# The four projections of a batch as three fp32r products, with the contexts split by GpSimd

## What is computed

```python
x = x + tanh(g_xattn[0]) * xattn(layernorm(x), ctx, ctx)      # 16 heads of 16 dimensions
x = x + tanh(g_ffn[0]) * moe(layernorm(x))                    # 8 experts, the best 2 of each token

def xattn(q, k, v):
    qh, kh, vh = q @ w_q.T + b_q, k @ w_k.T + b_k, v @ w_v.T + b_v    # the projections Q, K, V
    attn = softmax(qh @ kh.T / sqrt(16))                              # for each head
    return (attn @ vh) @ w_o.T + b_o                                  # the projection of the output
```

## Time and profile before

| what | value |
|---|---|
| median of 3 runs | 1241.16 us (1239.86 to 1241.84) |
| the profiled execution | 1240.26 us, span of its records 1238.4 us |
| granted TensorE clock, mean over the span | 0.959 of full |
| busy: PE, DVE, ACT, POOL | 1118.4, 643.7, 555.2, 312.8 us |
| instructions | 24933 |

### The profile page before, as it was taken

One profiled execution on the slowest core, in us unless ns is written; L12 is line 12 of the kernel. 1 busy time (PEld: TensorE's weight loads), 2 busy tenths in 40 slices (PEclk: granted clock), 3 DMA queues, 4 the chain that ended last, 5 costly groups with the idle time before them and its releaser, 6 DMA issues. The chain is left out here.

```text
span 1238.4 us, 24933 instructions
## 1 busy us (share of the span) xinstructions
PE 1118.4 (90%) x8725; PEld 949.4 (77%) x8725; DVE 643.7 (52%) x1524; ACT 555.2 (45%) x890; POOL 312.8 (25%) x366
## 2 busy tenths in 40 slices
PE   5789999999999998449999999999979999999994
PEld 4566666666666665326789999999948999999994
DVE  2546777776667766427643444444455444434442
ACT  3456666666666665236533333333354333333331
POOL 2122444444443332312212211121121221122111
PEclk8889999999999998669999999999989999999997
DMA  9100111011111101176342211221141221122111
GB/s 305 49 11 19 46 36 35 35 40 44 41 44 35 35 28 36 46 305 239 101 161 35 35 31 22 35 35 31 30 126 28 35 34 31 22 35 35 31 22 26
DMA packets 47642, 73.39 MB, mean 59 GB/s; under 512 B 6256, under 2 KB 42352, under 8 KB 44400
## 3 DMA queue, kind: packets, MB, share of 16 engines
q0 software_dynamic: 16896, 43.53, 13.7%
q1 hardware_dynamic: 29616, 28.21, 7.6%
q10 hardware_dynamic: 1088, 1.11, 0.3%
HBM read 47.66 MB, written 24.90 MB: 59 GB/s over the span
## 5 line engine op out<-in xcount | busy, mean ns | idle before, releaser
L1468 POOL DMA_INDIRECT out<-y,token x64 | 101.4, 1585 | 475.0 <-DVE y L1404 379.1
L1332 ACT ACTIVATE silu<-gate 128x512 f32<-128x512 f32 x128 | 76.5, 598 | 281.0 <-PE up L1241 281.0
L1398 DVE TENSOR_TENSOR h<-silu,up 128x512 f32<-128x512 f32 x128 | 88.0, 687 | 195.9 <-ACT silu L1332 195.9
L854 DVE TENSOR_REDUCE max_neg<-maxps 128x4 f32<-128x1024 f32 x128 | 156.4, 1222 | 58.3 <-PE maxps L468 56.7
L656 ACT ACTIVATE probs<-scores 128x1024 f32<-128x1024 f32 x128 | 131.8, 1030 | 68.1 <-PE scores L487 68.1
L1253 PE MATMUL down<-w_hi,h_hi 128*128 128x256 f32 x512 | 146.9, 287 | 0.0
L1253 PE MATMUL down<-w_hi,h_lo 128*128 128x256 f32 x512 | 144.1, 281 | 0.0
L1253 PE MATMUL down<-w_lo,h_hi 128*128 128x256 f32 x512 | 143.8, 281 | 0.0
L1400 DVE TENSOR_TENSOR h_lo<-h,h_hi 128x512 fp32r<-128x512 f32 x128 | 88.6, 692 | 89.4 <-ACT h_hi L1335 89.4
L1335 ACT ACTIVATE h_hi<-h 128x512 fp32r<-128x512 f32 x128 | 80.9, 632 | 96.5 <-DVE h L1398 96.5
L1241 PE MATMUL gate<-x_hi,w_hi 128*128 128x256 f32 x512 | 103.1, 283 | 0.0
(11 more groups left out here) (165 smaller groups left out, 2258.7 us busy)
## 6 DMA issues: line engine op xcount, KB each, us to landing
xg<-dispatched SPq DMA_DIRECT2D x41, 272.0 KB, 2.7
stage<-gate_T POOLq DMA_DIRECT2D x8, 1024.0 KB, 7.7
stage<-up_T POOLq DMA_DIRECT2D x8, 1024.0 KB, 9.6
stage<-down_T POOLq DMA_DIRECT2D x8, 1024.0 KB, 12.0
x_all<-x SPq DMA_DIRECT2D x16, 256.0 KB, 6.9
ctxT<-ctxT SPq DMA_DIRECT2D x16, 256.0 KB, 2.7
out<-x_all SPq DMA_DIRECT2D x16, 256.0 KB, 2.1
out<-y,token POOLq DMA_INDIRECT x72, 3.8
```

The source lines that it names most:

```text
L854: V.tensor_reduce(to, maxps[:], AX.X, ALU.max, negate=True).then_inc(s["max_taken"], 1)
L1332: nc.scalar.activation(silu[pair % 2][:], gate[pair % 2][:], ACT.Silu).then_inc(s_silu, 1)
L1398: V.tensor_tensor(h[pair % 2][:], silu[pair % 2][:], up[pair % 2][:], ALU.mult).then_inc(s_made, 1)
L1468: pool.indirect_dma_start(out, bass.IndirectOffsetOnAxis(token[:, t:t + 1], axis=0), y[:, t, :], None, compute_op=ALU.add).then_inc(s_adde ...
```

## The change

The weights of the four projections are split in the prologue, by VectorE, between the row maxima of the first batch; TensorE waits for all four before its first body. In the bodies V (except the first), K, Q and the output projection are twelve fp32r products each instead of four plain ones. The context is split by GpSimd at the head of its body. The high parts of the turned x and of the turned output are written by ScalarE where it copied them before, and the rests by VectorE, which reads the PSUM bank again and sets it free. In the loop SyncE waits for the split of an earlier context instead of for TensorE. `oT` goes; sixteen tensors are new in SBUF. Scores, softmax, routing and experts stay. The diff, cut to its core:

```diff
@@ SyncE, body @@
                 if ahead:
-                    sp.wait_ge(s["misc_written"], use.before)
+                    if isinstance(b, int):
+                        sp.wait_ge(s["misc_written"], use.before)
+                    else:
+                        sp.wait_ge(s["ctx_split"], b - 1)
                     load_ctx(b + 2, par)
@@ TensorE @@
+            def three_terms(high, rest, high2, rest2):
+                return [(l, r, c) for l, r in ((high, high2), (high, rest2), (rest, high2)) for c in range(HC)]
+
+            def project_in_parts(w, high2, rest2, what, use):
+                use.free(pe, what)
+                terms = three_terms(w_high[w], w_rest[w], high2, rest2)
+                for o in range(HC):
+                    for n, (l, r, c) in enumerate(terms):
+                        last = mm(use.bank(what)[:, o, :], l[:, c, o * P:(o + 1) * P], r[:, c, :], start=n == 0, stop=n == len(terms) - 1)
+                last.then_inc(s["misc_written"], 1)
...
+            def project_q_in_parts(use):
+                use.read(pe, "TX")
+                project_in_parts("q", x_high, x_rest, "Q", use)
+
+            def project_k_in_parts(b, par, use):
+                pe.wait_ge(s["ctx_split"], b - 1)
+                project_in_parts("k", c_high[par], c_rest[par], "K", use)
+
+            def project_v_in_parts(par, use):
+                rows_in_parts(c_high[par], c_rest[par], "v", "V", use)
@@ attn_out @@
                 use.read(pe, "TN")
-                use.free(pe, "WO")
...
+                rows_in_parts(o_high, o_rest, "o", "WO", use)
@@ before the bodies @@
+            pe.wait_ge(s["w_split"], 4)
             over_batches(pe, body)
@@ ScalarE @@
+            def high_of(to, what, made, use):
+                use.written(act, what)
+                nc.scalar.activation(to[:], use.bank(what)[:], ACT.Copy).then_inc(s[made], 1)
...
-                    read_whole(xT[:], "TX", use)
+                    high_of(x_high, "TX", "x_high_made", use)
                 exps(b, 2)
                 if back:
-                    read_whole(oT[:], "TN", use)
+                    high_of(o_high, "TN", "o_high_made", use)
@@ VectorE @@
+            def rest_of(b, to, high_, what, made, use):
+                dve.wait_ge(s[made], b)
+                V.tensor_tensor(to[:], use.bank(what)[:], high_[:].bitcast(fp32), ALU.subtract).then_inc(use.freed(what), 1)
+
+            def split_weights(n, what, raw):
+                V.tensor_copy(w_high[what][:], raw[:]).then_inc(s["w_high_made"], 1)
+                dve.wait_ge(s["w_high_made"], n + 1)
+                V.tensor_tensor(w_rest[what][:], raw[:], w_high[what][:].bitcast(fp32), ALU.subtract).then_inc(s["w_split"], 1)
@@ prologue, after the maxima of each pair @@
+                if pair >= 4:
+                    split_weights(pair - 4, "kvqo"[pair - 4], (wk_s, wv_s, wq_s, wo_s)[pair - 4])
@@ body @@
                 max_of_next(2)
+                if ahead:
+                    rest_of(b + 1, x_rest, x_high, "TX", "x_high_made", use)
+                if back:
+                    rest_of(b, o_rest, o_high, "TN", "o_high_made", use)
                 if late:
                     first_choice(b - 2)
                 max_of_next(3)
@@ GpSimd @@
+            def split_ctx(b, par):
+                if isinstance(b, int):
+                    pool.wait_ge(s["ctx_loaded"], b * 16 + 16)
+                else:
+                    alone.wait_ge(s["ctx_loaded"], b * 16 + 16)
+                G.tensor_copy(c_high[par][:], cT[par][:]).then_inc(s["ctx_high_made"], 1)
+                alone.wait_ge(s["ctx_high_made"], b - 1)
+                G.tensor_tensor(c_rest[par][:], cT[par][:], c_high[par][:].bitcast(fp32), ALU.subtract).then_inc(s["ctx_split"], 1)
@@ body @@
                 if ahead:
+                    if not is_first(b):
+                        alone.wait_ge(s["misc_written"], use.before - 3)
+                    split_ctx(b + 2, par)
                     scale_x(b + 2)
                     split(b + 2, "K", use, units_before(b) + (UNITS.index("K1") + 1 - len(UNITS)))
```

More of the change, by code:

```diff
@@ L123, in attention_stage @@
         wo_s = sb("wo_s", [P, HC, D])
+        w_high = {what: sb(f"w{what}_high", [P, HC, D], f32r) for what in "qkvo"}
+        w_rest = {what: sb(f"w{what}_rest", [P, HC, D], f32r) for what in "qkvo"}
+        c_high = [sb(f"ctx_high{i}", [P, HC, SEQ], f32r) for i in range(2)]
+        c_rest = [sb(f"ctx_rest{i}", [P, HC, SEQ], f32r) for i in range(2)]
+        x_high = sb("x_high", [P, HC, SEQ], f32r)
+        x_rest = sb("x_rest", [P, HC, SEQ], f32r)
+        o_high = sb("o_high", [P, HC, SEQ], f32r)
+        o_rest = sb("o_rest", [P, HC, SEQ], f32r)
         bq_s = sb("bq_s", [P, HC])
@@ L164, in attention_stage @@
         on = sb("on", [P, QT, D])
-        oT = sb("oT", [P, HC, SEQ])
         row = [sb(f"row{i}", [P, QT, ROW]) for i in range(2)]
@@ L201, in attention_stage @@
             rows_chain rows_ready scattered count_chain counted values_made
-            scale_chain scale2_chain""".split()
+            scale_chain scale2_chain ctx_high_made ctx_split w_high_made w_split
+            x_high_made o_high_made""".split()
         s = {n: sem(n) for n in names}
@@ L440, in project_v, with rows_in_parts @@
                 last.then_inc(s["misc_written"], 1)
+            def three_terms(high, rest, high2, rest2):
[7 more added lines that the diff above has]
+                last.then_inc(s["misc_written"], 1)
+            def rows_in_parts(high, rest, w, what, use):
+                use.free(pe, what)
+                terms = three_terms(high, rest, w_high[w], w_rest[w])
+                for t in range(QT):
+                    for n, (l, r, c) in enumerate(terms):
+                        last = mm(use.bank(what)[:, t, :], l[:, c, t * P:(t + 1) * P], r[:, c, :], start=n == 0, stop=n == len(terms) - 1)
+                last.then_inc(s["misc_written"], 1)
+            def project_q_in_parts(use):
[6 more added lines that the diff above has]
+                rows_in_parts(c_high[par], c_rest[par], "v", "V", use)
             def write_unit(n):
@@ L579, in stack_ahead @@
                         stack(b + 2, what[0], int(what[1]), unit(b, what))
-                if nxt:
+                if is_first(b):
                     project_v(1 - par, use)
+                elif nxt:
+                    project_v_in_parts(1 - par, use)
                 max_of_next(0)
@@ L590, in body @@
                 if ahead:
-                    project_k(b + 2, par, use)
+                    project_k_in_parts(b + 2, par, use)
                 score(b, par, 1)
@@ L611, in body @@
                 if ahead:
-                    project_q(use)
+                    project_q_in_parts(use)
                 max_of_next(5)
@@ L779, in _ @@
             over_batches(act, body)
-            read_whole(oT[:], "TN", EPILOGUE)
+            high_of(o_high, "TN", "o_high_made", EPILOGUE)
             second_weight(BATCHES - 2)
@@ L997, in _ @@
             norm_heads(b, 1, EPILOGUE)
+            rest_of(BATCHES, o_rest, o_high, "TN", "o_high_made", EPILOGUE)
             first_choice(b - 1)
```

## The result

| | before | after |
|---|---|---|
| median | 1241.50 us (1239.86 to 1242.87, 4 runs) | 1312.93 us (1311.18 to 1317.77, 4 runs) |
| the profiled execution | 1240.26 us, span 1238.4 | 1311.18 us, span 1309.3 |
| granted TensorE clock | 0.959 | 0.930 |

The ratio is 1.0585 (95% interval 1.0558 to 1.0613). The forecast was 1310 in a range of 1272 to 1328. A time "in the turn" counts from the first record of the turn's product V. Lines L... are those of the kernel in question.

The account below looks back on a forecast made before the run. TensorE was taken to bound the attention stage. To 1240.3 us came 14 x 3.0 = 42 for longer turns, 13 x 2.0 = 26 for the clock and 2.2 for edges: 70 more, 1310, range 1272 to 1328.

Parts of the forecast that it names:

- TensorE's gain: Projections as twelve fp32r products: 0.5 us less for K, Q and WO, 0.4 for V, 1.9 a turn.
- GpSimd: Context split ahead of scale_x delays xn and exponentials: 2.5 us stall before the second scores, which come 1.65 later.
- VectorE: Rests between maxima of pairs 2 and 3 delay WO, first_choice and masks: ranks 3.5 us late, turn 3.0 longer.
- the rule that I weighed: VectorE instructions with two SBUF inputs and GpSimd SBUF reads exclude each other; rests with a PSUM operand stay unaffected.
- The clock: TensorE's waits lower its clock in every turn: 2.0 us each in 13 turns, 26 us.
- the sign of being right: Attention stage: a turn of 32 to 35 us would show the forecast right.
- The edges: Prologue's last weight split 1.1 us, as much again for the first turn, last turns and epilogue 0: 2.2 us.
- No fall of the clock: Rival: attention turns lengthen but the clock stays up; 1285 us (1274 to 1303), chance 0.28.
- Only one chain is real: Rival: context split earlier or rests delay nobody; about 0.5 us a turn, 1247 to 1250, chance 0.11.
- The faster rival: TensorE's saving stands if first exponentials end by 258.9 and maxima 3 come early; 1212 us, chance 0.06.

Follow-up runs that it names:

- e2: Changed kernel with scale_x put before the split of the context on GpSimd, nothing else: 1281.83 us.
- e4: Changed kernel with only K and V in three fp32r products, Q and output projection plain, no rests on VectorE: 1271.19 us.
- e10: Changed kernel with contexts loaded one turn earlier, ahead of the transfers of the maxima, rests left in place: 1279.63 us.
- e8: Changed kernel with the two rests behind first_choice on VectorE, nothing else: 1288.63 us.
- e9: Changed kernel with contexts loaded a turn ahead and the rests behind first_choice, output projection in its old place: 1263.23 us.
- e1: Changed kernel with products nobody reads filling TensorE's waits before the second scores, maxima of pair 4 and ranks: 1290.80 us.
- e5: As e4, but each context loaded a turn ahead and only the weights of K and V split: 1237.85 us.
- e6: As e5, plus Q in parts with both parts of x made by GpSimd behind the split of K: 1238.22 us.
- e3: Changed kernel with only Q and output projection in parts; K and V plain, no context split, SyncE's old wait: 1290.38 us.
- e7: Changed kernel with contexts loaded a turn ahead, rests behind first_choice, output projection behind the scores of pair 4: 1261.35 us.
- e12: As e7, with products nobody reads in TensorE's two waits, before weighted values 0 and scores of pair 4: 1246.67 us.

## Why the prediction was right

Set beside turn 7, us into the turn:

| step | as predicted | measured |
|---|---|---|
| split of the context ends | 3.7 | 3.68 |
| `scale_x` begins | 3.9 | 3.76 |
| xn begins | 5.8 | 5.72 |
| second scores, after a wait of | 7.9, 2.5 | 7.77, 2.08 |
| output projection | 12.9 | 12.73 |
| maxima of pair 3 | 14.5 | 14.42 |
| waits before maxima of pair 4 and ranks | 1.1 and 1.1 | 0.83 and 0.90 |
| ranks | 17.2 | 17.10 |
| the turn, against before | +3.0 | +3.08 |

- **TensorE's gain.** This term was too large. Pairs of the new products start 0.24 us apart, 0.12 each, as taken from the earlier trace rows, but the first pair (except in V) and the step to the next group take 0.33 us each. From the start of the group to that of the next the output projection takes 1.63 us (300.50 to 302.13) and V 1.51 (287.77 to 289.28), where the plain ones took 1.93 and 1.82. Q takes 1.62, and K has the same spacing, though what follows it waits. That saves 0.3 us each, 1.2 a turn and not 1.9. The sum hardly shows it: part of what V and K did not save only made the wait before the second scores shorter (2.08 us for 2.5), the ranks came 3.38 us late for 3.5, and Q gave back 0.3 for 0.5.
- **GpSimd.** Right in order and size; e2 takes away its wait before the second scores, and e4 shows it by itself. The load starts 0.09 us earlier in turn 7 than before and no earlier in turn 6 (I had allowed 0.25), so the wait for TensorE was hardly what held it. What stood ahead of it were the transfers of the maxima: issued before them, 17 us into an earlier turn, it holds nothing up in the loop of e10.
- **VectorE.** The rests take 0.69 us. First_choice takes 1.69 (300.36 to 302.05, I took 1.75), and its last instruction 0.17, since POOL's K_rest had ended at 300.18. In e8 and e9 it stands under K_rest again and that instruction takes 0.99. The trace agrees with both sides of the rule that I weighed (Trainium skill, SBUF — State Buffer, Who interferes with whom): o_rest, with one operand in PSUM, ran beside K_rest (299.75 to 300.18) and was not longer, 0.69.
- **The clock.** The size was right and the form was not. I had one fall in each of 13 turns at 2.0 us. Twelve loop turns lost 24.6 us by the measure of turn 7, 2.05 each, and 21.5 by that of e1, 1.8 each. But the trace shows turn 7 without a fall, three turns at a clock of 0.86 (36.3 to 36.4 us), five at 0.90 (33.8 to 34.3) and three at 0.95, two of which (31.99 and 32.15) are hardly longer than turn 7. The three at 0.86 lie outside the 32 to 35 us that I had named as the sign of being right. The agreement of the mean owes something to luck: the price was a middle between two rows far apart.
- **The edges.** The first V starts 1.6 us later (1.1 predicted), of which TensorE's wait for the last weight split is 0.46; in e1 and e8, with the same prologue, V starts at 47.1 and 53.5 us, so the agreement says little. Turns 0 and 1 lost 5.6; by the sum they had 3.0 + 1.1 and 3.0 + 2.0, so 9.1. The tail lost 2.2 where I had 0. These misses cancel.
- **The rivals.** "No fall of the clock" had 1285, and e1, where the clock is held up, measures 1290.8: that case was priced rightly, and it was the clock that decided against it. "Only one chain is real" had 1247 to 1250; with one of the two eased the kernel is at 1280 or 1289, and each half of the change costs 31 or 50 us. That rival was wrong twice. It took 0.5 us a turn for the rests alone, from a delay of 2.3 at the output projection, which is about what the sum has there with the late scores in it (264.17 to 266.4). Its own case is e10, with the scores on time: there the ranks come 1.5 us late, 1.2 after what Q saves, and the turn is 2.9 longer. The rest of that is what the waits do to the clock. The faster rival asked for the exponentials to end by 5.4 us into the turn; e5, with the load early, has them at 5.85.

## What to carry to other kernels

Before work is given to an engine that has time to spare, look at what stands behind it in that engine's fixed order, and whether something short there starts the chain of the next stage. TensorE's time that a change saves counts only where the others are ready sooner too: e5 and e6 saved 0.6 and 0.9 us a turn on TensorE and kept 0.4 and 0.2. Time such a group from its start to the start of the next one: the spacing inside a dense row promised 0.5 us for each projection, and 0.3 came. And waits on TensorE can cost as much again by the clock (e10: 1.2 us a turn by its chain, and 1.7 more), so a change that adds such waits is priced with both.

## What the runs showed that I had not expected

- Nearly the same waits end in two ways. Turn 6 waits 2.29, 0.84 and 0.90 us and its clock falls twice; turn 7 waits 2.08, 0.83 and 0.90 us and it never falls. In e9 the wait before the output projection is 1.56 or 1.57 us in all twelve turns, nine with a fall and three without. In turns 6 to 11 of the changed kernel long and short turns alternate, 36.3 and 32.0 us. What decides between them the runs don't show.
- One wait of 2.0 to 2.3 us before the second scores left the clock of e4 at 1.00 in eight of twelve turns, while waits of 0.84 and 0.89 us with little between them pulled it down in every turn of e3, and 0.55 and 0.94 did in all but one of e7. The length of the longest wait does not tell whether the clock falls.
- Products without a reader made two kernels faster: 22 us in e1 and 15 in e12 over e7.
- Not tried: the early load alone, with plain products and no split, which would show what of e5 is the load's; the change with the old wait of SyncE; and filling on the kernel before.
